# A graph layer on one core: late products inside the first pass, paired half sums, and a second-pass end with fixed column windows

## The reference

```python
h = relu(layernorm(x))
m = relu(concat(h[src], edge_attr) @ W1 + b1) @ W2 + b2     # one row per edge
a = segment_sum(m, dst)                                     # pass 1
x = x + relu(concat(h, a) @ U1 + c1) @ U2 + c2
h = relu(layernorm(x))
x = x + segment_sum(h[src] * edge_weight[:, None], dst)     # pass 2
```

## Time and profile before

| | us |
|---|---|
| median of 3 runs | 2678.31 (2675.13 to 2681.2) |
| the profiled execution | 2659.47 |
| its span | 2657.7 |

### The profile page before, as it was taken

One profiled execution on the slowest core, in us unless ns is written; L12 is line 12 of the kernel. 1 busy time (PEld: TensorE's weight loads), 2 busy tenths in 40 slices (PEclk: granted clock), 3 DMA queues, 4 the chain that ended last, 5 costly groups with the idle time before them and its releaser, 6 DMA issues.

```text
span 2657.7 us, 57208 instructions
## 1 busy us (share of the span) xinstructions
PE 2049.9 (77%) x21651; PEld 1747.1 (66%) x21651; DVE 1311.2 (49%) x4334; ACT 974.0 (37%) x2419; POOL 1691.7 (64%) x1659
## 2 busy tenths in 40 slices
PE   5766666777777877777787777877778878999998
PEld 5555555656665666666666666766666767787886
DVE  6655555555555555556555555555555551111122
ACT  3334344444444444444444444444444441000111
POOL 6777777777777777777777777777777771000000
PEclk9988888888888888888888898889899899999998
DMA  3455444454444444334333333333223226999995
GB/s 88 129 169 173 162 159 159 165 171 140 142 140 148 130 132 135 118 119 127 106 109 113 99 97 94 87 94 85 74 74 82 65 62 240 401 377 384 372 350 163
DMA packets 422423, 414.27 MB, mean 156 GB/s; under 512 B 288562, under 2 KB 374178, under 8 KB 416000
## 3 DMA queue, kind: packets, MB, share of 16 engines
q1 hardware_dynamic: 369348, 354.89, 38.6%
q0 software_dynamic: 52064, 53.17, 8.8%
q10 hardware_dynamic: 732, 2.48, 0.4%
HBM read 258.64 MB, written 151.74 MB: 154 GB/s over the span
## 4 chain that ended last, share of the span: by engine, by line
POOL 62%; issue 19%; PE 9%; DMA 8%; DVE 1%; DVEq 0%; SPq 0%; ACT 0%; POOLq 0%
POOL rows L608 62%; DMA stage<-adjacency 7%; PE pair L1032 5%; PE pair L1039 1%; PE pair L1022 1%; PE pair L1045 1%; PE pair L864 1%; DMA x_all<-in_x_dram 1%; PE pair L852 0%; DVEq L1363 0%; PE pair L960 0%; PE pair L1053 0%; DVE nodes L1368 0%; DVE mean L1140 0%; SPq L490 0%
## 5 line engine op out<-in xcount | busy, mean ns | idle before, releaser
L608 POOL DMA_INDIRECT rows<-table,idx x1616 | 1649.4, 1021 | 512.0 <-issue 492.2
L721 ACT COPY stage<-pair 128x300 f32<-128x300 f32 x1616 | 622.3, 413 | 689.8 <-PE pair L946 687.3
L946 PE MATMUL pair<-bld 128*128 128x300 bf16 x4848 | 813.1, 316 | 4.5 <-DVE bld L1329 4.5
L923 PE MATMUL pair<-w1b,rings 128*128 128x128 f32 x1616 | 307.1, 349 | 530.4 <-DVE rings L1305 530.3
L923 PEld LDWEIGHTS pair<-w1b,rings 128*128 128x128 f32 x1616 | 261.2, 246 | 588.3 <-DVE rings L1305 587.9
L946 PEld LDWEIGHTS pair<-bld 128*128 128x128 bf16 x4848 | 552.2, 120 | 134.7 <-DVE bld L1329 7.9
L1329 DVE TENSOR_TENSOR bld<-bld,part 128x512 bf16<-128x512 bf16 x1212 | 432.4, 410 | 0.0
L1323 DVE TENSOR_TENSOR bld<-iota_lo,lo 128x512 bf16<-128x512 f16 x404 | 172.5, 427 | 471.1 <-PE pair L946 468.3
L1325 DVE TENSOR_SCALAR bld<-iota_key,key 128x300 bf16<-128x300 f16 x1616 | 383.5, 300 | 0.0
L1305 DVE TENSOR_TENSOR rings<-rows,pair 128x512 f32<-128x512 f32 x202 | 138.3, 685 | 461.4 <-DMA rows<-table,idx 461.4
L1032 PE MATMUL pair<-stage,h 125*64 125x96 f32 x5870 | 297.4, 253 | 25.0 <-DMA stage<-adjacency 22.2
(11 more groups left out here) (131 smaller groups left out, 779.3 us busy)
## 6 DMA issues: line engine op xcount, KB each, us to landing
stage<-adjacency SPq DMA_DIRECT2D x270, 480.0 KB, 9.4
rings<-in_edge_attr_dram SPq DMA_DIRECT2D x202, 256.0 KB
adjacency<-stage SPq DMA_DIRECT2D x28, 1200.0 KB
rows<-table,idx POOLq DMA_INDIRECT x1616
adjacency<-stage SPq DMA_DIRECT2D x20, 1080.0 KB
adjacency<-stage SPq DMA_DIRECT2D x20, 960.0 KB
adjacency<-stage SPq DMA_DIRECT2D x20, 840.0 KB
adjacency<-stage SPq DMA_DIRECT2D x20, 720.0 KB
```

The source lines that it names most:

```text
L608: pool.indirect_dma_start(out=rows[:, slot, t, :], out_offset=None, in_=table, in_offset=bass.IndirectOffsetOnAxis(ap=idx[:, g, t:t + 1], ...
L721: act.copy(tiles[:, g % STAGE, :, t * WT:(t + 1) * WT], build_bank[i % 3][:, 0:KEYS].rearrange("p (h w) -> p h w", w=WT)).then_inc(tile_ke ...
L923: last = pe.matmul(bank[:, a * P:(a + 1) * P], eaT[:, slot, a, :], w1b2[:, :], start=True, stop=True)
L946: last = pe.matmul(build_bank[i % 3][:, 0:KEYS], hot_w[q % 2][k][:, :, u], hot_key[q % 2][:, u, :], start=(k == 0), stop=(k == PARTS - 1))
```

## The change

1. **Late products.** A (chunk, quad) pair, where a quad is four groups or two batches, whose chunk was not ready when the quad was built, is multiplied inside pass 1 once it is: SP loads 4 x 240 columns of `adjacency` (480 KB, `load_late`), PE makes 5 matmuls of 192 columns (`late`), DVE adds the result to the quad's partial result in SBUF (`keep_late`), which SP has loaded and stores back (96 KB each way). At most two such products stand in a step, none in the four steps from a chunk's `SUMMED` on. By the tables of the program there are 207, in 105 steps (102 of them with two), from step 29 on. They use 2 slots for loads (`LATE`) and 4 for sums (`BACK`).
2. **What is left for the end.** 29 batches have one chunk left and 72 have two; before, the number fell from ten to one. These are 173 (batch, chunk) pairs where there were 587, 865 matmuls for 2935, and 101 piece loads for 317. `direct` is unchanged in amount (2115 matmuls).
3. **Order and size of the end.** The partial result is added by DVE while it copies the bank (`keep_u` moves from ACT to DVE) and the identity matmul goes. The columns of a batch are fixed by its number (62 further for each batch, 144 wide), so DVE adds once, with no address from a register; its one-hot matrix is 144 wide, not 80. The place offsets are worked out at the start, with further tests.
4. **Half sums in pass 1.** `sum_hid` makes 8 matmuls of 64 columns of `hid` whose results alternate between the upper and lower half of the partitions; DVE adds 128 partitions and leaves the two halves apart, and `make_g` multiplies with weights that stand twice. The edge count comes from a `tensor_reduce` on DVE (`sum_hot`) and one more matmul, and is added by a second DVE instruction on one row. `sum_hid` moves behind all tiles and `turn_ea`.
5. **Start.** POOL clears 33 more partitions of `nodes` (6250 columns) ahead of the two memsets that were there, and the second of these now has 128 partitions for 65.

The core of the diff:

```diff
@@ sp
-                sp.dma_start(partial[b, :, :], s_stage[:, n % 2, :]).then_inc(s_stored[n % 2], 16)
+                sp.dma_start(sums_of(b, 1), s_stage[:, n % 2, :]).then_inc(s_stored[n % 2], 16)
+            def load_late(n, c, q, fresh):
+                if fresh:
+                    for slot in range(STAGE):
+                        sp.wait_ge(adj_stored[slot], 16 * (q + 1))
+                wait_count(sp, late_done, n - LATE + 1)
+                sp.dma_start(late_piece[:, n % LATE, :].rearrange("p (g w) -> p g w", g=QUAD),
+                             adjacency[QUAD * q:QUAD * q + QUAD, :, c * CW:(c + 1) * CW].rearrange("g p w -> p g w")
+                             ).then_inc(late_loaded[n % LATE], 16)
...
+                    sp.dma_start(late_sum[n % BACK], sums_of(2 * q, 2)).then_inc(late_back[n % BACK], 16)
+            def store_late(n, q):
+                sp.wait_ge(late_kept, n + 1)
+                sp.dma_start(sums_of(2 * q, 2), late_sum[n % BACK]).then_inc(late_stored[n % BACK], 16)
@@ gpsimd
+            pool.memset(nodes[D:DEG + 1, 0:N], 0.0).then_inc(pool_step, 1)
+            pool.wait_ge(pool_step, 4)
             pool.memset(hT[D:D + 1, :], 1.0).then_inc(ones_set, 1)
             pool.wait_ge(ones_set, 1)
-            pool.memset(acc1[:, :], 0.0).then_inc(consts_set, 1)
+            pool.memset(sums1[:, :], 0.0).then_inc(consts_set, 1)
@@ tensor
-                segment(sum_bank, hid, slot, slot, D + 1).then_inc(group_done, 1)
+                for t in range(T):
+                    pe.matmul(half_of(sum_bank, t)[:, 0:W], hid[:, slot, t, 0:D], hot[:, slot, t, :],
+                              start=(t < 2), stop=(t >= T - 2))
+                wait_step(pe, hot_summed, g)
+                pe.matmul(sum_bank[D:P, W:2 * W], ones[:, 0:D], hot_sum[:, slot, :], start=True,
+                          stop=True).then_inc(group_done, 1)
...
+            def late(s):
+                for i, (n, c, q) in enumerate(LATE_AT.get(s, [])):
+                    if i == 0:
+                        wait_count(pe, late_kept, n)
+                        wait_count(pe, x1_made, sum(SUMMED[k] < s for k in range(CHUNKS)))
+                    pe.wait_ge(h2_staged, c + 1)
+                    pe.wait_ge(late_loaded[n % LATE], 16 * (n // LATE + 1))
...
@@ vector
-                dve.tensor_tensor(to, to, sum_bank[0:D + 1, 0:W], ALU.add).then_inc(acc_added, 1)
+                dve.tensor_tensor(to, to, sum_bank[:, 0:W], ALU.add)
+                dve.tensor_tensor(count, count, sum_bank[DEG:DEG + 1, W:2 * W], ALU.add).then_inc(acc_added, 1)
+            def sum_hot(g):
+                wait_step(dve, hot_made, g)
+                dve.tensor_reduce(hot_sum[:, g % TWO, :], hot[:, g % TWO, :, :].rearrange("p t w -> p w t"), AX_X,
+                                  ALU.add).then_inc(hot_summed, 1)
```

More of the change, by code:

```diff
@@ L420, in gathered_wait, with sums_of, back_loads @@
                 eng.wait_ge(gathered[slot], ((g - slot) // RING + 1 + turns) * 16 * T)
[L422 to L424 removed]
+        def sums_of(b, n):
+            return partial[:, b * COLS:(b + n) * COLS]
+        def back_loads(n):
+            return sum(LATE_FRONT[i] is not None or ready_for(2 * LATE_QUAD[i]) > 0
+                       for i in range(n % BACK, n + 1, BACK))
         def half_of(bank, i):
```

266 lines of the change are left out of this document (198 added, 68 removed).

## The result

| | before | after |
|---|---|---|
| median of 4 runs | 2676.7 us | 2443.9 us (2431.0 to 2449.0) |
| profiled execution, its span | 2659.5, 2657.7 us | 2431.0, 2429.2 us |
| ratio | | 0.912, 95% interval 0.910 to 0.915 |

What follows compares the result with a forecast made beforehand. POOL's gathers were taken to bound the kernel up to the last gather, then DMA and later PE. 2659.5 - 245 - 2 + 3 + 2.7 = 2418 us profiled; with 18.8 us for the median 2437 us, range 2412 to 2460.

Steps and rivals of the forecast that it cites:

- start: first gather later: At the start, one more POOL memset holds a small DVE instruction later: +3 us, between 0 and +5.3 us.
- pass 1: first to last gather: In pass 1, late products are hidden by waits for gathered rows: 0 us; uncovered, up to 194 us.
- hand-over: last gather's end to first product: Between pass 1 and the end, PE's two products of step 201 and SP's wait for their stores: +2.7 us (2 to 6).
- the end, first to last product: In the end, 29 batches at 1.35 us, 72 at 1.82 us and nine chunk turn-overs: 176 us for 421.
- the tail: Behind the last product, register reads leave a chain of dependent adds: 11 us for 13, -2 us (0 to -4).
- The large term: In the end, 173 (batch, chunk) pairs for 587 and cheaper batches at PE's pace: -245 us.
- DMA or a latency bounds the end: Rival for the end: batches at 2.14 and 1.7 us, +33 us, 2470 us; chance 0.12.
- the bounds of 165 and 199 us: For the end: 165 us at 1.70 and 1.25 us a batch, 199 us with all loads at 252 GB/s.
- The landing of 5.5 us: In pass 1, the time a late product's load takes to land, taken between bounds of 4.0 and 9.4 us.
- its sign for a fall: In pass 1, an idle stretch of 3.03 us puts PE at 1.2 GHz for a while: sums take 1.92 us, not 1.09.
- what DVE does to POOL now is 0.08 us a gather: In pass 1, DVE's effect on gathers, read from 0.94 us for one gather against the mean of 1.021 us.
- "wrong" list: Signs against it: POOL waiting, PE idle before late loads, steps over 10.6 us, DVE held over 5 us, end batches over 2 us.

Runs made afterwards that it cites:

- Experiment 2: The changed kernel with one slot instead of two for the late products' loads: 2728.5 us, ratio 1.020 to the kernel before.
- experiment 1: The changed kernel with only chunk 0's 7 late products, 573 chunk products left for the end: 2657.5 us, ratio 0.995 to the kernel before.
- experiment 9: The kernel before, unchanged, run once more for its trace: 2672.3 us, ratio 0.999; profiled span 2679.4 us, mean gather 1.032 us.
- experiment 10: The changed kernel with the half sums undone (65-column sums, no reduction, second add or count product): 2461.0 us, ratio 0.919 to the kernel before.
- experiment 12: The changed kernel with 26 identity products keeping TensorE busy across the hand-over: 2443.1 us, ratio 0.913 to the kernel before.
- experiment 3: The changed kernel with eight buffers instead of four for the end's partial results: 2433.3 us, ratio 0.911 to the kernel before.
- experiment 11: The changed kernel with at most one late product a step, 128 in all and 331 chunk products in the end: 2510.4 us, ratio 0.937 to the kernel before.

## Why the prediction was right, step by step

The sum for the profiled execution was 2418 us and came out at 2431.0:

| step | forecast | measured | off by |
|---|---|---|---|
| start: first gather later | +3 | 63.25 to 65.64 us, +2.4 | -0.6 |
| pass 1: first to last gather | 0 | +6.8 | +6.8 |
| hand-over: last gather's end to first product | +2.7 | 18.8 to 22.8 us, +4.0 | +1.3 |
| the end, first to last product | 176 | 184.4 | +8.4 |
| the tail | 11 | 8.0 | -3.0 |

That is 12.9 of the 13.0 us. The median stands 12.9 us above the profiled execution where 18.8 us were taken from before, and that brings 13 down to 7 us on the median (2443.9 for 2437). That part of the agreement is luck: how far a profiled execution lies from its median is scatter. The large term stands on its mechanism: the end came out 237 us shorter for a forecast of 245.

- **The end** was right in its mechanism, and two errors in its size cancel in part. A batch at PE's pace takes 1.58 and 1.09 us and not 1.82 and 1.35, because `turn_u` takes 0.36 us and `put` 0.24 where 0.43 and 0.39 were taken from the earlier trace rows; the products' 0.98 us is as forecast. At those paces and with nine turn-overs (0.83 us each) the end would take 153 us. Waits for loads and the low clock at its start add 31 us, which the sum had no term for; the rival "DMA or a latency bounds the end" named them. One-chunk batches took a mean of 1.51 us in place of 1.35. The end fell where the forecast put it between the bounds of 165 and 199 us.
- **Late products** cost what was worked out (2.0 us for two, 1.9 forecast) and are hidden. Experiment 2 shows the bound, and how near it lay: with one slot PE's wait is 4.1 us a step and the kernel is slower than before. The landing of 5.5 us was no measured number. In experiment 2 the 102 second loads reach their product 3.3 to 4.4 us behind their issue, so it was too long, to the safe side, and of the two bounds the one from free queues (4.0 us) was near.
- **The clock** between 1500 and 2000 us rose to 0.95 where PE had more work and was 0.87 where it hadn't (experiment 1), as the prediction had it. But its sign for a fall, an idle stretch of 3.03 us, is no rule: in the same trace of before a wait of 3.23 us has no such tail.

```profile
2008.14 1.16 PE L923 MATMUL pair<-w1b,rings 128*128 128x128 f32 x8 [3.23 <-DVE rings L1305]
...
2009.90 1.09 PE L929 MATMUL pair<-hot,rings 128*65 128x40 f32 x16
```

- **Half sums**: the PE side, -0.2 us a step, is about right (0.67 + 0.29 us for 1.09). The DVE side was mis-sized: the reduction takes 0.77 us (no more than 0.69 was allowed), and all the extras 1.7 us a step (0.20 + 0.77 + 0.36 + 0.35) for 1.2, still under the bound of 2.1. The weak step is "what DVE does to POOL now is 0.08 us a gather", a mean taken as a property of the work. It is mostly a matter of when a gather starts against VectorE's instructions with both inputs in SBUF (experiment 9). That the new instructions hold no gather themselves, as the prediction took it, was right. The 17.9 us that go with the half sums (experiment 10) had no term, and 17 us of scatter between executions had none either. In the profile on record of before the count happened to be low (34 against 51), and that alone can hide such a gain: pass 1 looks 6.8 us longer with the change, but against the second execution of before after's last gather is 8.7 us earlier.
- **Start**: the hold at 17.8 us stayed and a second one came, as forecast. In the traces of experiments 10 and 12, with the same start, the first gather comes at 64.31 us, so of the 2.4 us half is scatter:

```profile
17.84 3.18 DVE L1271 TENSOR_SCALAR mean<-row_sum 125x5 f32<-125x5 f32 x1
21.05 5.34 POOL L703 MEMSET nodes<- 128x6290 f32 x1
...
23.00 3.48 DVE L1271 TENSOR_SCALAR mean<-row_sum 125x5 f32<-125x5 f32 x1
```

- **The signs**: the last gather was to be near 2206 us (2212.8), the gather near 1.02 us (1.025), late products never waiting (0.4 us in all), PE's waits for gathered rows about 1 us a step (456.0 us over 202 steps, 2.3 us each, and 1.4 us behind two late products), the clock above 0.91 (0.95 in the last window but 0.86 and 0.89 before), the first product near 2229 us (2236.8), batches of 1.8 and 1.35 us (1.96 and 1.51 with their waits). No sign of the "wrong" list appeared except batches of the end over 2 us, and of these there are 32 of 101.

## What to carry to other kernels

Work that a bandwidth-bound last stage does at its limit can be moved into an earlier stage whose pace another engine sets, and it costs nothing there as long as each transfer is issued a full step ahead; one buffer less turned the whole gain into a loss. The first units taken out are worth the most: 0.61 us each while DMA bounds the end, 0.46 where PE nears it. Before a mean duration is used as a price, look at its spread: 34 or 51 gathers of 1.95 us among 1616 are 17 us between two executions of one program.

## What the runs showed of the hardware

- An indirect gather of 128 rows issued by POOL takes 0.94 us, but 1.95 or 2.28 us if it starts 0.02 to 0.06 us ahead of a run of three or four VectorE instructions with both inputs in SBUF. Of the gathers over 1.0 us, 455 of 461 end 0.79 to 0.84 us behind the end of a VectorE instruction (experiment 9).
- A small VectorE instruction (125x5) that takes 0.17 us alone was held by POOL's arithmetic and memset for up to 7.84 us; each hold of over 3 us ended within 0.03 us of the end of a POOL instruction.
- TensorE's granted clock fell early in the end although the engine was over 0.9 busy: to 0.50 for over 40 us (experiment 3), to 0.78 and 0.91 for 20 us each (after), and to 0.66 for 20 us after the idle 4 us ahead of it had been filled (experiment 12). With batches of three chunks it was 0.91 and then 1.00 (experiment 11).
- In one job the kernel took 950 us longer between its first gather and its end, with three engines standing still together, and there a change of 8.8% was worth nothing.
